# A graph layer's neighbour sums: counts from a ones column, strips joined without TensorE

## What is computed

```python
xn = layernorm(x)
# graph part: mean of the neighbours' rows, two products, relu
summed = segment_sum(xn[src], dst)                  # 212500 rows gathered
counts = segment_sum(ones, dst)
agg = summed / maximum(counts, 1.0)[:, None]
gnn = relu(agg @ W_l.T + b_l + xn @ W_r.T) + xn
# mixing part: linear attention over all nodes, feature map elu(v) + 1
q, k, v = feature(xn @ wq + bq), feature(xn @ wk + bk), xn @ wv + bv
mix = (q (k^T v) / (q . sum(k) + 1e-6)) @ wo + bo
x = x + gnn + mix
# expert part: the two best of 8 experts by the mean row, gelu, layer norm
y = layernorm(x)
x = x + layernorm(w1 * expert1(y) + w2 * expert2(y) + y) * gamma + beta
```

## Time and profile before

| | |
|---|---|
| median of 3 runs | 2990.27 us (2988.75 to 2993.2) |
| the profiled execution, its own time | 2991.13 us |
| its span, first to last instruction | 2989.4 us |
| busy: PE, PEld, DVE, ACT, POOL | 2472.3, 1613.1, 1723.5, 773.9, 1738.7 us |
| DMA: moved, mean rate | 327.01 MB, 109 GB/s |
| chain of waits that ended last, by engine | PE 44%, POOL 22%, DVE 15%, issue 12%, DMA 4%, ACT 2% |

### The profile page before, as it was taken

How to read it: one execution, slowest core, us unless ns; L and a number is a source line. 1 busy time by engine, 2 the same in 40 slices (tenths; PEclk the granted TensorE clock), 3 DMA queues, 4 the chain that set the end, 5 groups by cost and what they waited for, 6 DMA issues and landing times.

```text
span 2989.4 us, 38538 instructions
## 1 busy us (share of the span) xinstructions
PE 2472.3 (83%) x11532; PEld 1613.1 (54%) x11532; DVE 1723.5 (58%) x3602; ACT 773.9 (26%) x1810; POOL 1738.7 (58%) x1731
## 2 busy tenths in 40 slices
PE   6888778878787887778787878878787879999998
PEld 5765344444443444444344444444444469999997
DVE  7885454455445545554554455455445557777777
ACT  4553011111111111111111111111111145565564
POOL 5546777777777777777777777777777600000000
PEclk9998777777877777777778787777777789999999
DMA  4333344444444444443444444444434322222212
GB/s 145 101 110 94 115 124 122 115 125 123 122 116 125 123 116 122 124 125 114 123 124 120 117 125 125 114 123 124 124 114 125 104 66 82 66 63 76 71 63 66
DMA packets 192238, 327.01 MB, mean 109 GB/s; under 512 B 32703, under 2 KB 138216, under 8 KB 192200
## 3 DMA queue, kind: packets, MB, share of 16 engines
q0 software_dynamic: 80160, 219.14, 25.9%
q1 hardware_dynamic: 111624, 107.01, 11.5%
q10 hardware_dynamic: 416, 0.39, 0.1%
HBM read 275.21 MB, written 51.20 MB: 109 GB/s over the span
## 4 chain that ended last, share of the span: by engine, by line
PE 44%; POOL 22%; DVE 15%; issue 12%; DMA 4%; ACT 2%; DVEq 0%; POOLq 0%; ACTq 0%; SPq 0%
POOL ring L643 22%; PE pd L1108 9%; PE pd L987 7%; PE pa L1048 6%; PE pd L1014 6%; PE pa L1093 5%; PE pc L1093 4%; DMA ring<-xn_table,idxb 4%; PE pc L1065 2%; DVE bst L1156 2%; PE pc L975 2%; DVE nh L1183 1%; DVE nv L1178 1%; DVE ohh L1306 1%; ACT yT L656 1%
## 5 line engine op out<-in xcount | busy, mean ns | idle before, releaser
L643 POOL DMA_INDIRECT ring<-xn_table,idxb x1661 | 1607.8, 968 | 509.8 <-issue 490.3
L1048 PE MATMUL pa<-ring,ohh 128*128 128x512 f16 x1661 | 765.6, 461 | 225.5 <-DMA ring<-xn_table,idxb 211.5
L1326 DVE TENSOR_REDUCE ring<-pa 128x256 f32<-128x512 f32 x196 | 135.3, 691 | 585.9 <-PE pa L1048 585.2
L1065 PEld LDWEIGHTS pc<-ohh,ones_h 128*1 128x1 f16 x2045 | 134.2, 80 | 533.4 <-issue 533.4
L1065 PE MATMUL pc<-ohh,ones_h 128*1 128x128 f16 (+1 forms) x2045 | 384.3, 219 | 0.0
L1048 PEld LDWEIGHTS pa<-ring,ohh 128*128 128x128 f16 x1661 | 172.9, 104 | 352.3 <-issue 172.5
L1108 PE MATMUL pd<-parts 128*128 128x256 f32 (+1 forms) x1568 | 312.1, 282 | 1.8 <-DVE parts L1496 1.8
L1306 DVE TENSOR_TENSOR ohh<-iota_f,edges 128x512 f16<-128x512 f32 (+1 forms) x391 | 272.8, 718 | 0.9 <-issue 0.9
L969 PE MATMUL pd<-work,KS_s 128*128 128x256 f32 x196 | 100.7, 668 | 199.5 <-DVE work L1360 199.5
L1108 PEld LDWEIGHTS pd<-parts 128*128 128x128 f32 (+1 forms) x1568 | 253.0, 188 | 10.3 <-DVE parts L1496 2.5
L741 ACT ACTIVATE work<-pd 128x512 f32<-128x512 f32 (+1 forms) x49 | 29.2, 596 | 884.3 <-PE pd L953 884.3
(11 more groups left out here) (188 smaller groups left out, 3479.3 us busy)
## 6 DMA issues: line engine op xcount, KB each, us to landing
ring<-xn_table,idxb POOLq DMA_INDIRECT x1661, 2.7
yT<-in_x SPq DMA_DIRECT2D x24, 512.0 KB, 4.0
xn_table<-ring SPq DMA_DIRECT2D x24, 512.0 KB, 4.8
work<-in_x SPq DMA_DIRECT2D x48, 256.0 KB
x_rows<-work SPq DMA_DIRECT2D x48, 256.0 KB
y_rows<-work SPq DMA_DIRECT2D x48, 256.0 KB
work<-y_rows SPq DMA_DIRECT2D x24, 512.0 KB, 4.3
work<-x_rows SPq DMA_DIRECT2D x24, 512.0 KB, 3.9
```

The source lines that it names most:

```text
L643: pool.indirect_dma_start(out=msgs[:, k, :, :].rearrange("p s d -> p (s d)"), out_offset=None, in_=xn_table[:, :], in_offset=bass.Indirect ...
L1048: ins = mm(pa[:, t % 2, :], oh[:, slot, :], msgs[:, k, :, :].rearrange("p s d -> p (s d)"), start=begins, stop=ends, skip_group_check=True)
L1065: ins = mm(pc[0:1, v, c0:c1], ones_h[:, 0:1], oh[:, slot, o0:o1], start=first, stop=closing, skip_group_check=True)
L1326: V.tensor_reduce(strips[:, (NS * u + t + 1) % KEPT, :], pa[:, t % 2, :].rearrange("p (s d) -> p d s", s=PARTS), AX.X, ALU.add)\
```

## The change

Seven things change together.

- In stage 1 the factor XS goes into the reciprocal root and so into the normalised rows: POOL's scaling falls away, ACT copies the high part without a factor. The weights of the keys are divided by XS ahead of stage 1, the row factors and the key sums behind it.
- A slot of `msgs` has 514 half-precision columns in place of 512, the last two are ones, set once, after the table's stores have landed.
- PE multiplies each tile's one-hot with the 256 high columns and then with the 256 low columns and a one, both into the same 257 columns of PSUM. So the parts are added there and column 256 is the count. The separate counting falls away.
- The one-hot columns are taken modulo 128 (`iota_f` is 64 longer and read from column 0 or 64), so that a node has the same partition in each of the two strips that hold it.
- ACT takes the strips out of PSUM. DVE joins them by three additions of half the partitions, takes the reciprocals of two columns of counts, and ACT scales the sums with them.
- PE turns the scaled sums by four transposes in place of the join by products, and the spreading falls away.
- PE's dense pieces are cut in halves and put at other tiles (`DENSE`), the batches are cut so that none crosses a strip, and `batch_used` is signalled for the last batch too.

```diff
-    BATCH = [(0, 4), (4, 8), (8, 12), (12, 17), (17, 21), (21, 25), (25, 29), (29, 34)]
+    BATCH = [(0, 4), (4, 8), (8, 13), (13, 17), (17, 21), (21, 25), (25, 30), (30, 34)]
...
+    SW = D + 2
+    assert all(len(set(LO[k0:k1])) == 1 for k0, k1 in BATCH)
...
+        SLOT = PARTS * D + 2
+        MSGS = TB * SLOT // 2
+        msgs = ring[:, 0:MSGS].bitcast(F16).rearrange("p (k r) -> p k r", r=SLOT)
+        strips = ring[:, MSGS:MSGS + KEPT * SW].rearrange("p (n d) -> p n d", d=SW)
+        assert MSGS + KEPT * SW <= RING
...
-                pool.wait_ge(s["xn_ready"], q + 1)
-                wait(pool, s["lo_made"], q)
-                pool.sem_inc(s["waits_taken"], 1)
-                for v, n in whole(q):
-                    ins = pool.tensor_scalar(xs[0:n, v, :], xnb[u][0:n, v, 0:D], XS, None, ALU.mult)
-                ins.then_inc(s["xs_made"], 1)
-                pool.wait_ge(s["xs_made"], q + 1)
...
-                    ins = pool.tensor_tensor(xp[u][0:n, v, D:2 * D], xs[0:n, v, :], xp[u][0:n, v, 0:D], ALU.subtract)
+                    ins = pool.tensor_tensor(xp[u][0:n, v, D:2 * D], xnb[u][0:n, v, 0:D], xp[u][0:n, v, 0:D], ALU.subtract)
...
-                            out=msgs[:, k, :, :].rearrange("p s d -> p (s d)"), out_offset=None, in_=xn_table[:, :],
+                            out=msgs[:, k, 0:PARTS * D], out_offset=None, in_=xn_table[:, :],
...
-                    ins = nc.scalar.activation(xp[u][0:n, v, 0:D], xnb[u][0:n, v, 0:D], ACT.Copy, scale=XS)
+                    ins = nc.scalar.activation(xp[u][0:n, v, 0:D], xnb[u][0:n, v, 0:D], ACT.Copy)
...
+            def take_strip(b, t, u):
+                act.wait_ge(s["batch_used"], NBT * b + 2 * t + 3)
+                nc.scalar.activation(strips[:, (NS * u + t + 1) % KEPT, 0:D + 1], pa[:, t % 2, 0:D + 1], ACT.Copy)\
+                    .then_inc(s["strip_taken"], 1)
+            def scale_sums(d, u):
+                act.wait_ge(s["cnt_rec"], d + 1)
+                for g in range(2):
+                    own = strips[:, NS * u + 2 * g + 1, 0:D]
+                    ins = nc.scalar.activation(own, own, ACT.Copy, scale=cnts[:, g:g + 1])
+                ins.then_inc(s["strips_scaled"], 1)
...
+                first = is_int(b, 0)
...
+                def numbers(*qs):
+                    for q in qs if more else ():
...
+                if is_int(b, NB):
+                    scale_sums(b - 1, 1 - u)
...
+                    return
+                block_xn(b)
+                numbers(0, 1)
+                take_strip(b, -1, u)
+                if not first:
+                    scale_sums(b - 1, 1 - u)
+                numbers(2)
+                take_strip(b, 0, u)
+                block_xnT(b)
+                block_queries(b)
+                if not first:
+                    block_y(b - 1)
+                numbers(3, 4)
+                take_strip(b, 1, u)
+                if not first:
+                    block_yT(b - 1)
+                numbers(5, 6, 7)
+                take_strip(b, 2, u)
...
+            def queries(d, o):
...
+                for c in range(C):
+                    ins = mm(pd[:, 1, o * BN:(o + 1) * BN], wq_s[:, c, o * P:(o + 1) * P],
+                             xT2[:, c * BN:(c + 1) * BN], start=c == 0, stop=c == C - 1)
+                if o == C - 1:
+                    ins.then_inc(s["q_made"], 1)
+            def normalizers(d, c):
...
+                ins = mm(pd[:, 0, c * BN:(c + 1) * BN], KS_s[:, c, :], pq[:, c * BN:(c + 1) * BN],
+                         start=True, stop=True)
+                if c == C - 1:
+                    ins.then_inc(s["nrm_made"], 1)
+            def product(a, w, at, d, h):
...
+                    ins = mm(pd[:, 2 + h, at:at + D], a[:, c * BN + h * P:c * BN + (h + 1) * P], w[:, c, :],
+                             start=a is xT2 and c == 0, stop=a is not xT2 and c == C - 1, skip_group_check=True)
+                return ins
+            def root_product(d, h):
...
+                product(xT2, wrT, 0, d, h)
+            def mixed_product(d, h):
+                pe.wait_ge(s["qhat_made"], d + 1)
+                product(pq, M_s, D, d, h)
+            def neighbour_product(d, h):
+                pe.wait_ge(s["agg_taken"], d + 1)
+                ins = product(aggS, wlT, 0, d, h)
+                if h == 1:
+                    ins.then_inc(s["o_made"], 1)
...
-            def strip_sums(b):
-                return [t for t in range(-1, NS) if not (is_int(b, NB - 1) and LO.index(STRIP * t) >= LAST)]
-            def join_strips(d, u):
-                sums = strip_sums(d)
-                pe.wait_ge(s["strip_taken"], NS * d + len(sums))
+            def turn_sums(d, u):
+                pe.wait_ge(s["strips_scaled"], d + 1)
...
-                for t in sums:
-                    c0, c1 = max(STRIP * t, 0), min(STRIP * t + P, BN)
+                for g in range(2):
...
-                        ins = mm(pd[:, 0, c * BN + c0:c * BN + c1], strips[:, (NS * u + t + 1) % KEPT, c * P:(c + 1) * P],
-                                 ident[:, c0 - STRIP * t:c1 - STRIP * t], start=t == -1 and c == 0, stop=t == sums[-1],
-                                 skip_group_check=True)
+                        ins = nc.tensor.transpose(pd[:, 0, c * BN + g * P:c * BN + (g + 1) * P],
+                                                  strips[:, NS * u + 2 * g + 1, c * P:(c + 1) * P], ident[:, :])
...
-            JOIN = 6
-            HOOKS = ((11, products, 1), (11, turn_xn, 0), (13, queries, 0), (22, normalizers, 0), (26, turn_y, 1))
+            DENSE = {1: (root_product, 0, 1), 2: (root_product, 1, 1), 3: (mixed_product, 0, 1),
+                     4: (mixed_product, 1, 1), 12: (neighbour_product, 0, 1), 13: (neighbour_product, 1, 1),
+                     16: (queries, 0, 0), 17: (queries, 1, 0), 24: (normalizers, 0, 0), 25: (normalizers, 1, 0)}
+            TURN_SUMS, TURN_X, TURN_Y = 9, 14, 27
+            def dense(b, k, u):
+                late = not is_int(b, 0)
+                if k == TURN_SUMS and late:
+                    turn_sums(b - 1, 1 - u)
+                if k == TURN_X:
+                    turn_xn(b)
+                if k == TURN_Y and late:
+                    turn_y(b - 1)
+                if k in DENSE:
+                    work, part, back = DENSE[k]
+                    if late or not back:
+                        work(b - back, part)
...
-                    spread_counts(b - 1, 1 - u)
-                    join_strips(b - 1, 1 - u)
-                    products(b - 1)
+                    for part in (root_product, mixed_product):
+                        for h in range(2):
+                            part(b - 1, h)
+                    turn_sums(b - 1, 1 - u)
+                    for h in range(2):
+                        neighbour_product(b - 1, h)
...
-                        if k == JOIN and not is_int(b, 0):
-                            spread_counts(b - 1, 1 - u)
-                            join_strips(b - 1, 1 - u)
-                        for at_tile, work, back in HOOKS:
-                            if k == at_tile and not (back and is_int(b, 0)):
-                                work(b - back)
+                        dense(b, k, u)
...
+                        if is_int(b, 0) and k == 0:
+                            pe.wait_ge(s["ones_set"], 1)
+                        mm(pa[:, t % 2, 0:D], oh[:, slot, :], msgs[:, k, 0:D], start=begins, stop=False, skip_group_check=True)
+                        ins = mm(pa[:, t % 2, 0:D + 1], oh[:, slot, :], msgs[:, k, D:2 * D + 1], start=False, stop=ends,
+                                 skip_group_check=True)
+                    if ks:
...
-                then(V.tensor_scalar(v, mv[:, 0:k, 1], EPS, None, ALU.add))
+                then(V.tensor_scalar(v, mv[:, 0:k, 1], EPS, factor ** -2, ALU.add, ALU.mult))
...
-                          rstd_a[:, bass.ds(q * QT, len(tiles))], nmr_a[:, bass.ds(q * QT, len(tiles))], fill)
+                          rstd_a[:, bass.ds(q * QT, len(tiles))], nmr_a[:, bass.ds(q * QT, len(tiles))], fill, XS)
...
-            V.tensor_copy(iota_f[:, :], iota_i).then_inc(s["iota_float"], 1)
+            V.tensor_copy(iota_f[:, WIN:WIN + STRIP], iota_i[:, 0:STRIP])
+            V.tensor_copy(iota_f[:, 0:WIN], iota_i).then_inc(s["iota_float"], 1)
...
+            V.tensor_scalar(wk_s[:, :, :], wk_s[:, :, :], 1.0 / XS, None, ALU.mult).then_inc(s["wk_scaled"], 1)
...
-            V.tensor_copy(kx_s, pc[:, :, 0:KXW]).then_inc(s["kx_taken"], 1)
+            V.tensor_scalar(rstd_a[:, 0:GT], rstd_a[:, 0:GT], 1.0 / XS, None, ALU.mult)
+            V.tensor_scalar(nmr_a[:, 0:GT], nmr_a[:, 0:GT], 1.0 / XS, None, ALU.mult).then_inc(s["rows_unscaled"], 1)
+            V.tensor_copy(kx_s[:, :, D:KXW], pc[:, :, D:KXW])
+            V.tensor_scalar(kx_s[:, :, 0:D], pc[:, :, 0:D], 1.0 / XS, None, ALU.mult).then_inc(s["kx_taken"], 1)
...
+            dve.wait_ge(s["xn_stored0"], quad_dmas(NQ, 0))
```

(61 more changed lines are left out.)

75 lines of the change are left out of this document (5 added, 70 removed).

## The result

The changed kernel takes 2997.41 us (median of 8, 2995.67 to 3002.99), the kernel before, run beside it on the same chip, 2990.72 us (8 runs, 2987.67 to 2996.44): a ratio of 1.0023 [1.0012, 1.0034]. It is 6.7 us slower, a small difference of 0.2% but outside the spread of the runs, where a gain of 17 us was forecast. It lies 1.4 us above the range of 2950 to 2996. The profiled execution of the change took 2995.67 us for a span of 2994.2 us.

What follows compares the result with a forecast made beforehand. POOL's own issue of 1661 gathers, 1.25 us each with the pause, was taken to bound the gathering piece, DVE's chain stage 1. Terms -16 - 1.8 + 5 - 5 = -17.8 us took 2991.1 to 2973 us, range 2950 to 2996.

Steps and rivals of the forecast that it cites:

- Step 5: Gathering piece: three new two-input DVE adds per block and moved DVE phases, between -36 and +63 us, taken as +5.
- Rival A: Gathering piece: the adds make gathers longer, deciding above 1.2 us excess per block; 3005 us at 1.5; chance 0.12.
- Rival D: Gathering piece: PE becomes the bound through a low clock, 0 to 92 us, about 3060 us; chance 0.03.
- Steps 3 and 4: Gathering piece: counts by a ones column with 1028 B rows, and strips taken by ACT, each forecast to change nothing.
- Step 1: Stage 1: POOL's scaling goes, freeing 0.83 us per period of DVE's chain; 11.4 to 18.3 us, taken as -16.
- step 2: End of stage 1: POOL's last subtraction follows ACT at once, so the first gather starts 1.8 us earlier.
- rival B: Stage 1 gains little, as PE or the x rows bound it; period near 10, about 2986 us; chance 0.13.
- Step 6: Tail: from last gather to middle part, shorter by 5 us, between 2 and 8.

Runs made afterwards that it cites:

- e13: The kernel before, unchanged, profiled once more: 2998.62 us, excess of the gathers 44.0 us.
- e4: The changed kernel with slots 1280 B apart in place of 1028 B: 3000.39 us, excess 75.2 us.
- e2: The changed kernel with the one-hots' iota read from PSUM: 2966.47 us, ratio 0.9924 to the kernel before.
- e14: The changed kernel with one PSUM input for one-hots, residual bias, middle part's first sum and last query product: 2949.61 us, ratio 0.9857 to the kernel before.
- e1: The kernel before with only the change's stage 1 (scaled rows): 2970.80 us, ratio 0.9939 to the kernel before.
- e3: The changed kernel without the three DVE adds that join the strips (output incomplete): 2995.11 us, excess 68.9 us.
- e15: The changed kernel with PE's dense pieces whole, at the tiles of the kernel before: 3009.76 us, excess 84.1 us.
- e17: The changed kernel with one unread 128-column count matmul per tile added on PE: 3001.20 us, excess 73.4 us.
- e18: The changed kernel with four unused 0.69 us DVE reductions per block standing in for the strips: 2992.07 us, excess 64.9 us.
- e5: The kernel of e14, run on the slower device: 3432.93 us, ratio 0.8763 to the kernel before.
- e12: The changed kernel with the old stage 1, on the slower device: 3451.11 us, excess 70.5 us.
- e9: The kernel of e5 again on the slower device: 3436.72 us, ratio 0.8773 to the kernel before, excess 17.0 us.

## Why the prediction was wrong

**Step 5 failed, and with it the sign.** It took "+5, as nothing says that the new phases are better or worse", and that step was the mistake: something did say it. By its own formula for random starts the instructions of the kernel before would cost 1.8 us per block, 89 us in all; they cost 36.5. (As a start within 0.04 us of the gather's holds nothing, my estimate of the random value is nearer 77 us before and 86 after.) The old kernel stood well below it, so whatever shifts DVE's instructions can be expected to take them back towards it, and only by luck keeps them.

The traces have it so: of the 632 instructions of 0.4 us or more with two SBUF inputs in the gathering piece before, 205 cross a gather's start (181 in e13), where random starts would give 272; after the change it is 276 of 778, against 310. The step's reason for the discount, that PE's releases put "most of them" just behind a gather's start, holds in part: 244 of the 632 start in the third of a microsecond behind one, where random starts would give 165. After the change 155 of 778 do, against 200, so that discount is gone.

Every version of the new gathering piece with its inputs left in SBUF came out between 62 and 84 us, on either device. That this is a return to the random value fits all of them, but is an argument, not a test. The adds themselves were sized right: 7.6 us against "10 us at random, 4 us at the same discount". What was missing were the 27 us of the old instructions. The range of step 5, -36 to +63, held the measured +34.5; the range of the forecast did not reach there.

Rival A is what happened, and its bound is confirmed: it was to decide at 1.2 us of excess per block, and at 1.45 it decided. Its sign, a mean gather above 0.98 us, came at 0.989. Its mechanism was half right, since it blamed the adds. Its chance of 0.12 was low for the same reason. Rival D did not come: POOL waited 1.5 us for PE, although PE's clock in the piece was 0.74.

**The reading beneath it holds.** POOL's 1.25 us per gather set the piece, and work taken off PE and DVE was worth nothing: 459 and 133 us less there, and no gain. Steps 3 and 4 at zero stand (e4 for the stride; ACT's strips in this group of the page of after, 0.38 us each, never on POOL's path):

```profile
L737 ACT ACTIVATE ring<-pa 128x257 f32<-128x257 f32 x196 | 74.3, 379 | 917.9 <-PE pa L1075 917.2
```

The Trainium skill (SBUF — State Buffer, "Who interferes with whom") states that a VectorE instruction with two SBUF inputs contends with a GpSimd one that reads SBUF. A gather has its indices there (`idxb`), and e2 and e14 agree: 71.0, 45.3, 24.2 us of excess as inputs move to PSUM. The same section infers that a tensor_tensor leaves descriptor generation alone; the gather of 1.19 us beside L1374, a tensor_tensor, speaks against that. That it is the reading of the indices which waits is argued from this, not shown.

**Step 1 was undersized.** Forecast -16, and -17.8 with step 2; measured -20.8 up to the first gather. A period fell from 10.12 to 9.19 us, from L1186 to L1186 (DVE, 121 to 135 us of after):

```profile
124.88 1.41 DVE L1186 TENSOR_SCALAR nv<-mv 128x4 f32<-128x4 f32 x1
...
134.07 1.40 DVE L1186 TENSOR_SCALAR nv<-mv 128x4 f32<-128x4 f32 x1
```

That is 0.93 us per period, more than the 0.83 of the one held instruction, in 22 periods 20.5 us. Why the period fell by more than that instruction was not followed up. (PE's margin, which rival B puts at 0.7 us, is 9.3 - 8.4 = 0.9 us by the step's own numbers.) The stall that should go is gone, and the one that should stay stayed, only behind the subtraction that is now L619 and was L624. The groups of DVE from 88 to 240 us, against the earlier trace rows:

```profile
L1186 DVE TENSOR_SCALAR nv<-mv 128x4 f32<-128x4 f32 x15 | 21.0, 1401 | 0.5
...
L1191 DVE SCALAR_TENSOR_TENSOR nh<-nh,nv 128x4 f32<-128x4 f32 x45 | 7.3, 162 | 1.6
```

The end of stage 1, against the earlier trace rows, has ACT's last part and POOL's last step back to back, as step 2 said, but it gained 0.8 us and not 1.8. From the end of ACT's part to the first gather it is 6.5 us (7.3 before), as that gather now starts 5.1 us behind POOL's last step, where it was 4.1. So step 1 alone is 20.0 of the 20.8 us:

```profile
235.98 0.72 ACT L672 ACTIVATE ring<-yT 128x256 f16<-128x256 f32 x2
236.78 1.29 POOL L619 TENSOR_TENSOR ring<-yT,ring 128x256 f16<-128x256 f32 x2 [0.38 <-ACT ring L672]
...
243.19 1.03 POOL L638 DMA_INDIRECT ring<-xn_table,idxb  x1 [5.11 <-issue]
```

**Step 6 came out, and a faster clock on top of it**: -5 forecast, 9.2 measured for the whole tail. Against the earlier trace rows:

```profile
2397.00 1.89 PE L990 MATMUL pd<-M_s,work 128*128 128x256 f32 x8
...
2399.29 0.66 PE L1026 MATMUL pd<-ident,ring 128*128 128x128 f32 x4 [0.40 <-ACT ring L744]
...
2400.08 0.69 DVE L1349 COPY work<-pd 128x512 f32<-128x512 f32 x1 [1.78 <-PE pd L1026]
...
2402.86 0.69 DVE L1354 TENSOR_TENSOR work<-pd,bl_b 128x512 f32<-128x512 f32 x1 [2.09 <-PE pd L990]
```

The middle part starts 11.7 us behind the last gather's end at 2391.2, not 16. About 4 us of that are not the new tail's: e1, with the old tail, is at 16.8 us (21.3 before, 21.6 in e13), with PE's granted clock in the tail at 0.67 in place of 0.58. Against e1 the new tail gains 5.1 us, the 5 of the step. The same 16 join matmuls in e1:

```profile
2373.84 2.05 PE L1009 MATMUL pd<-ident,ring 128*128 128x64 f32 x16
```

They took 3.78 us in the earlier trace rows. Why the clock was higher was not tried, nor whether it is all of the 4 us.

**What stays open.** No single part of the new gathering piece was found to be what moved the old phases: not the adds (e3), the pieces (e15), the tile without its count product (e17), nor the strips' going alone (e18). The batches' new cuts, which set when the one-hot builds start, and ACT's place in the chain were not tried alone. Each change of order shifts several groups at once. Nor is it known what slows the second chip, whether it is one, and why versions of the change are 12% or more faster than the kernel before there.

## What to carry to other kernels

Where one engine's instruction is stretched by whoever overlaps its start, compare the stretch in the trace with what random starts would cost. If it stands well below, count a return towards the random value as a likely cost of a rearrangement. And don't look for better phases: take the cause away. Here one input of the instructions in question was moved to an idle PSUM bank, and 48 us came out of a kernel without any change to the work of its critical engine.

## What the runs showed that I had not expected

- Repeated profiles of the same kernel differ by 7.5 us in the excess (e13), and the time follows one to one. A single execution of this kernel says nothing below that.
- Taking three adds per block away gained 2 us (e3), and adding four VectorE instructions of 0.69 us per block cost nothing measurable (e18, 2992.1 against 2995.7 us).
- The same kernel takes about 2990 us in most runs and about 3916 us beside e5 to e12, on another chip or in another condition. e9, among the latter, has the same 0.95 us per gather and a clock of 0.78.
- The hold has a sharp edge: an instruction that starts 0.05 us before the gather holds it until it ends, and one that starts 0.03 us before it doesn't hold it at all.
